# First attention of a two-layer decoder: all four groups in paired steps, the convolution's heads between the turns of the last

## The reference

```python
x = x + L0_attn(layernorm(x))            # 16 heads of 16, LoRA weights, softmax
x = x + L0_xattn(ctx, ctx, layernorm(x)) # long convolution of ctx*ctx products, times q
x = x + L0_ffn(layernorm(x))             # LoRA experts, top 2 of 8
x = x + L1_attn(layernorm(x))            # 16 heads of 128
x = x + L1_xattn(layernorm(x), ctx, mask)
x = x + L1_ffn(layernorm(x))             # 32 routed experts
```

```python
q, k, v = [x @ W.T + b for W, b in ...]          # x: (16, 128, 256), 16 heads of 16
p = softmax(q @ k.T / 4); out = p @ v
x = x + out @ Wo.T + bo
```

## Time and profile before

| | us |
|---|---|
| median of 3 runs (lowest, highest) | 953.66 (953.63, 954.13) |
| the profiled execution | 953.93 |
| its span in the profile | 952.10 |
| TensorE busy in the span | 927.0 (97%) |
| VectorE, ScalarE, GpSimd busy | 620.6, 481.0, 239.7 |

### The profile page before, as it was taken

One profiled execution on the slowest core, in us unless ns is written; L12 is line 12 of the kernel. 1 busy time (PEld: TensorE's weight loads), 2 busy tenths in 40 slices (PEclk: granted clock), 3 DMA queues, 4 the chain that ended last, 5 costly groups with the idle time before them and its releaser, 6 DMA issues.

```text
span 952.1 us, 20014 instructions
## 1 busy us (share of the span) xinstructions
PE 927.0 (97%) x7627; PEld 790.5 (83%) x7627; DVE 620.6 (65%) x1380; ACT 481.0 (51%) x1614; POOL 239.7 (25%) x261
## 2 busy tenths in 40 slices
PE   9999999999999999999999999999999999999988
PEld 7777778899788888888888888888888887777767
DVE  5878777897865576564456464546546665777864
ACT  4988877444445554443444353444444554434632
POOL 2656796671011111111111111011111123101000
PEclk9999999999999999999999999999999999999999
DMA  7100000002430000000000000020003001200002
GB/s 287 68 2 2 2 2 2 2 1 92 136 130 1 2 1 1 1 1 1 1 1 1 2 1 1 1 62 1 1 1 90 1 1 68 113 2 2 2 2 89
DMA packets 11325, 28.02 MB, mean 29 GB/s; under 512 B 1856, under 2 KB 7264, under 8 KB 10720
## 3 DMA queue, kind: packets, MB, share of 16 engines
q1 hardware_dynamic: 10512, 26.48, 7.9%
q10 hardware_dynamic: 720, 0.27, 0.1%
HBM read 24.65 MB, written 2.10 MB: 28 GB/s over the span
## 4 chain that ended last, share of the span: by engine, by line
PE 86%; DVE 9%; issue 2%; ACT 2%; POOL 1%; DVEq 0%; POOLq 0%; ACTq 0%
PE bank L50 15%; PE bank L52 14%; PE bank L51 14%; PE bank L2294 6%; PE bank L2243 5%; PE bank L421 3%; PE bank L431 3%; PE bank L2284 3%; PE bank L2167 2%; PE bank L2158 2%; PE bank L180 2%; PE bank L443 2%; PE bank L1702 2%; PE bank L1133 1%; PE bank L1151 1%
## 5 line engine op out<-in xcount | busy, mean ns | idle before, releaser
L2099 POOL TENSOR_TENSOR wa_prob<-wa_prob,wa_rsum 128x512 f32<-128x512 f32 x64 | 67.6, 1057 | 405.1 <-DVE wa_rsum L2682 405.1
L2476 ACT ACTIVATE wa_prob<-wa_prob,wa_negmax 128x128 f32<-128x128 f32 x256 | 100.1, 393 | 66.5 <-DVE wa_negmax L2671 66.2
L50 PE MATMUL bank<-norm_xT_hi,wide_hi 128*128 128x512 f32 x256 | 105.9, 414 | 0.2 <-DVE norm_xT_lo L191 0.2
L51 PE MATMUL bank<-norm_xT_lo,wide_hi 128*128 128x512 f32 x256 | 101.0, 395 | 0.0
L52 PE MATMUL bank<-norm_xT_hi,wide_lo 128*128 128x512 f32 x256 | 101.0, 395 | 0.0
L2738 DVE TENSOR_TENSOR wa_z_lo<-bank,wa_z_hi 128x512 fp32r<-128x512 f32 x64 | 44.3, 692 | 86.8 <-ACT wa_z_hi L2510 86.3
L646 ACT ACTIVATE v_prob<-bank,la_negmax 128x128 f32<-128x128 f32 x256 | 91.3, 384 | 13.6 <-DVE la_negmax L733 13.6
L2484 ACT COPY wa_q<-bank 128x512 f32<-128x512 f32 x64 | 37.6, 588 | 93.5 <-PE bank L52 93.5
L2491 ACT COPY wa_v<-bank 128x512 f32<-128x512 f32 x64 | 37.4, 586 | 89.2 <-PE bank L52 89.2
L353 POOL TENSOR_TENSOR v_prob<-v_prob,la_rsum 128x512 f32<-128x512 f32 x64 | 66.8, 1043 | 47.2 <-DVE la_rsum L738 47.1
L2294 PEld LDWEIGHTS bank<-wa_probT,wa_v 128*128 128x128 f32 x512 | 65.4, 191 | 10.7 <-DVE wa_probT L2725 5.0
(11 more groups left out here) (287 smaller groups left out, 2363.6 us busy)
## 6 DMA issues: line engine op xcount, KB each, us to landing
wide_raw<-in_wide_w SPq DMA_DIRECT2D x16, 512.0 KB, 6.9
em_w<-in_em_w SPq DMA_DIRECT2D x1, 4096.0 KB, 13.7
lc_kt<-in_ctx_rev SPq DMA_DIRECT2D x1, 2048.0 KB, 10.8
lc_toep<-in_toeplitz SPq DMA_DIRECT2D x1, 2048.0 KB, 14.5
li_kt<-in_ctx_rev SPq DMA_DIRECT2D x4, 512.0 KB, 6.8
out_x<-x SPq DMA_DIRECT2D x8, 256.0 KB, 2.5
x<-in_x SPq DMA_DIRECT2D x3, 512.0 KB, 5.0
h_or_w<-in_li_w SPq DMA_DIRECT2D x1, 1024.0 KB, 5.0
```

The costliest lines, as they stand in the source:

```text
L50: nc.tensor.matmul(out, a[0], b[0], start=start, stop=False, skip_group_check=True)
L51: nc.tensor.matmul(out, a[0], b[1], start=False, stop=False, skip_group_check=True)
L2099: nc.gpsimd.tensor_tensor(prob[:, s], prob[:, s], rsum[:, s, :].unsqueeze(2).to_broadcast([P, G, P]), ALU.mult).then_inc(prob_ok, 1)
L2476: last = nc.scalar.activation(prob[:, s, j, :], prob[:, s, j, :], ACT.Exp, bias=negmax[:, s, j:j + 1], scale=SCALE, accum_out=sums[:, s, j ...
```

## The change

All four groups are now taken in pairs on TensorE. The separate loop for the last group is gone. In a pair of the last group (p = 0 to 7) two convolution heads, 2p and 2p + 1, stand between the two turns, the even one in `b_p[0]`, the odd one in `b_p[1]`. Behind every second pair stands a projection (11 to 14), behind pairs 4 and 6 a turn of x for the convolution stage, all three kinds in `b_p[1]`: so an odd head also waits for the addition to x (`x_ok`) of the projection before it, or for the copy of the turned x. ScalarE copies both heads of a pair in the even step, behind the exponentials.

VectorE's order in the last group becomes that of the others: the copy of the turn first, then the row maximum, which also loses its special place at the start of a group. Additions and the splits of x move by a step at three places. The power and the application of the norm move one step later, (7, 8) to (8, 9), 6 to 7. Eight skips move from group 1 to the last group. In groups 1 and 2 the queries' first product moves from behind pair 0 to between the turns of pair 1, in groups 0 and 1 the first turn of the next x from behind pair 4 to between the turns of pair 5. A projection now comes ahead of what else stands between two turns. In group 0 the second turn of x moves from behind pair 0 to between the turns of pair 1.

```diff
-    STATS_AT, VAR_AT, POWER_AT, APPLY_AT, BIAS_AT = (3, 5), 6, 6, (7, 8), 10
+    STATS_AT, VAR_AT, POWER_AT, APPLY_AT, BIAS_AT = (3, 5), 6, 7, (8, 9), 10
...
-    TURN_0 = (10, 13)
+    TURN_PAIRS = (4, 6)
...
     def hi_due(n):
 
-        return batch_due(n, RG) if n <= PAIRED else batch_due(n, HI_AT) if n > PAIRED + RG else None
+        return batch_due(n, RG)
...
         def between(g, p):
 
             t = g + 1
-            if p == 2:
+            if p == 1 and g > 0:
+                pe.wait_ge(norm.s_lo, DC * norm.split(t))
+                q_or_k(t, 0, 0, b_p[0], q_ps)
+            elif p == 5 and t + 1 < NG:
+                pe.wait_ge(k_ok, DC * t + 2)
+                turn_x(t + 1, 0, b_p[0])
+            elif p == 2:
...
         def first_conv(h):
 
+            p, second = divmod(h, 2)
             if h == 0:
                 pe.wait_ge(v_ok, 2 * NG)
                 pe.wait_ge(kk_first, 2 * CONV_C)
-            else:
-                pe.wait_ge(c_ok, h)
+            wait(pe, c_ok, h - 1)
+            if second:
+                if p - 1 in TURN_PAIRS:
+                    pe.wait_ge(norm.s_hi, DC * (norm.done(NG) - 1) + TURN_PAIRS.index(p - 1) + 1)
+                elif p % 2 == 0:
+                    pe.wait_ge(x_ok, NB - 5 + p // 2)
+                else:
+                    pe.wait_ge(x_ok, NB - 5)
             pe.wait_ge(pr.skip_ok, h + 1)
-            conv_head(pr, 0, h, b_p[0]).then_inc(c_ps, 1)
+            conv_head(pr, 0, h, b_p[second]).then_inc(c_ps, 1)
+
+        def behind_last(p):
+
+            pe.wait_ge(c_ok, 2 * p + 2)
+            if p in TURN_PAIRS:
+                c = TURN_PAIRS.index(p)
+                pe.wait_ge(x_ok, NB - 3 + c)
+                turn_x(NG, c, b_p[1])
+            elif p % 2 == 1:
+                project(NB - 5 + p // 2)
...
-        for n in range(0, PAIRED, 2):
+        for n in range(0, N, 2):
             g, u = divmod(n, U)
             p = u // 2
-            late = n >= 2 * 2
             turn(n)
-            if late:
-                between(g, p)
+            if n == 0:
+                scores(n + RG)
+                pe.wait_ge(v_ok, 1)
+                turn_x(1, 0, b_p[0])
+            elif n == 2:
+                pe.wait_ge(norm.s_lo, DC * norm.split(0) + 1)
+                turn_x(1, 1, b_p[0])
+                scores(n + RG)
+            elif g < NG - 1:
                 b = project_due(n + 1)
                 if b is not None:
                     project(b)
+                between(g, p)
             else:
-                scores(n + RG)
-            if n == 0:
-                pe.wait_ge(v_ok, 1)
-                turn_x(1, 0, b_p[0])
+                first_conv(u)
+                first_conv(u + 1)
             turn(n + 1)
-            if late:
+            if 2 < n < N - RG:
                 scores(n + RG)
             weigh(n)
             weigh(n + 1)
-            behind(g, p)
-        for n in range(PAIRED, N + 1):
...
+            if g < NG - 1:
+                behind(g, p)
+            else:
+                behind_last(p)
...
         def keep_first_conv(h):
             act.wait_ge(c_ps, h + 1)
-            conv_keep(pr, 0, h, b_p[0]).then_inc(c_ok, 1)
+            conv_keep(pr, 0, h, b_p[h % 2]).then_inc(c_ok, 1)
...
-            if N - U < n <= N:
-                keep_first_conv(n - (N - U) - 1)
+            if PAIRED <= n < N and u % 2 == 0:
+                keep_first_conv(u)
+                keep_first_conv(u + 1)
...
-            if g in (1, 2) and u % 2 == 1:
-                if g == 1 and u == 1:
+            if g == 2 and u % 2 == 1:
+                if u == 1:
                     dve.wait_ge(pr.conv_loaded, 16 * 4)
-                add_skip(pr, 8 * (g - 1) + u // 2)
+                add_skip(pr, u // 2)
+            if g == NG - 1 and u < CONV_H // 2:
+                add_skip(pr, CONV_H // 2 + u)
...
-            opens = n < PAIRED and 0 < g and u == 0
-            if n < PAIRED:
+            if n < N:
                 keep_probT(n)
...
-                if n > 1 and n % U == 1:
-                    row_max(n + 2)
-                if not opens:
-                    row_max(n + 3)
+            if n + 3 < N:
+                row_max(n + 3)
...
```

More of the change, by code:

```diff
@@ L494, in behind @@
             t = g + 1
[L495 to L499, removed]
+            if g == 0 and p == 1:
                 pe.wait_ge(norm.s_lo, DC * norm.split(t))
                 q_or_k(t, 0, 0, b_p[0], q_ps)
-            elif p == first + 1:
+            elif p == (2 if g == 0 else 1):
                 pe.wait_ge(q_ok, DC * t + 1)
                 q_or_k(t, 0, 1, b_p[0], k_ps, (0,))
-            elif p == 4 and t + 1 < NG:
-                pe.wait_ge(k_ok, DC * t + 2)
-                turn_x(t + 1, 0, b_p[0])
             elif p == 5:
@@ L585, in tensor_program @@
             weigh(n + 1)
-            behind(g, p)
-        for n in range(PAIRED, N + 1):
[L588 to L597, removed]
-            if PAIRED < n:
-                weigh(n - 1)
-            b = batch_due(n, PROJECT_AT)
-            if b is not None:
-                project(b)
-            if n < N and not first:
-                extra(g, u)
-            if PAIRED < n and u % RG != 1:
-                first_conv(n - PAIRED - 1)
+            if g < NG - 1:
+                behind(g, p)
+            else:
+                behind_last(p)
         pe.wait_ge(exp_ok, N)
@@ L659, in extra @@
             if t == NG:
-                if u - 1 in TURN_0:
-                    norm.hi_chunk(act, NG, TURN_0.index(u - 1), b_p[1], pr.xe)
+                if u // 2 - 1 in TURN_PAIRS and u % 2 == 0:
+                    norm.hi_chunk(act, NG, TURN_PAIRS.index(u // 2 - 1), b_p[1], pr.xe)
                 return
@@ L666, in extra @@
                 norm.hi_chunk(act, t, 1, b_p[0], xT[t % 2][0])
-            elif u == 10 and t + 1 < NG:
+            elif u == 11 and t + 1 < NG:
                 norm.hi_chunk(act, t + 1, 0, b_p[0], xT[(t + 1) % 2][0])
@@ L712, in scalar_program @@
             b = hi_due(n)
-            if b is not None and n <= PAIRED:
+            if b is not None:
                 keep_o(b)
@@ L722, in scalar_program @@
                 extra_late(g, u)
-            b = hi_due(n + 1)
-            if b is not None and n >= PAIRED:
-                keep_o(b)
-            if N - U < n <= N:
-                keep_first_conv(n - (N - U) - 1)
+            if PAIRED <= n < N and u % 2 == 0:
+                keep_first_conv(u)
+                keep_first_conv(u + 1)
     def vector_program(dve, ahead):
@@ L833, in vector_program @@
                     norm.lo_chunk(dve, 1, 0, b_p[0], *xT[1])
-                if n == 3:
+                if n == 2:
                     norm.lo_chunk(dve, 1, 1, b_p[0], *xT[1])
-                if n > 1 and n % U == 1:
-                    row_max(n + 2)
-                if not opens:
-                    row_max(n + 3)
+                if u == 11 and g + 2 < NG:
+                    norm.lo_chunk(dve, g + 2, 0, b_p[0], *xT[g % 2])
+            if n + 3 < N:
+                row_max(n + 3)
             b = hi_due(n)
```

15 lines of the change are left out of this document (2 added, 13 removed).

## The result

| | before | after |
|---|---|---|
| median us (lowest, highest) | 953.66 (953.07, 954.13) | 957.70 (956.97, 958.34) |
| span of the profiled execution | 952.10 | 956.0 |
| TensorE busy | 927.0 | 925.0 |
| VectorE, ScalarE, GpSimd busy | 620.6, 481.0, 239.7 | 620.1, 480.5, 236.7 |

The ratio after to before is 1.0038, 95% interval [1.0027, 1.0049], which does not contain 1. The forecast was 953.6, from 950.6 to 956.2. TensorE is busy for 2 us less and the kernel takes 4 us more, so waits were added.

What follows compares the result with a forecast made beforehand. TensorE was taken to set the pace in the first attention. From 953.93, 2.2 saved in the first three groups, 2.1 lost in the last and 0 behind it gave 953.8, less the profile-to-median difference 953.6 us; range 950.6 to 956.2.

Steps and rivals of the forecast that it cites:

- the front: First three groups: five moves together to save 2.2 us, from 0.6 to 3.0.
- The new waits ahead of heads 5, 9, 13: Last group: these heads wait for the addition emptying their bank, 1.47 each with the fresh start, 4.4 us together.
- TensorE's own work, pairing: Last group: without new waits, paired steps take 35.24 us instead of 38.98, a gain of 3.7.
- the turn of x: Last group, first turn of x behind pair 4: waits 0.9 us for the later normalisation, 0.1 to 1.6.
- Skips "fill VectorE's idle time": Eight skips moved from group 1 to the last group fill VectorE's idle time there, with no cost charged.
- The queries' move: Groups 1 and 2: first product between the turns of pair 1 saves 0.3 us each, 0.6 together.
- The power: Group 0: power at step 7 instead of 6 lets step 8's normalisation go first, saving a 0.5 us GpSimd wait.
- GpSimd's other waits: First three groups: VectorE work moved from ahead of reciprocals saves 0.9 of 1.9 us, from 0 to 1.5.
- The start: Group 0: second turn of x and its split a step earlier, ahead of a maximum, remove a 0.2 us wait.
- Behind the last weighing: VectorE's first convolution product starts 1.7 us after the last weighing, as before: 0, from -0.2 to +1.4.
- B: Last group, slower rival: late head copies on ScalarE delay exponentials and a later turn; 956.4 us, chance 0.22.
- the first three groups saved under 1 us: Sign of error named beforehand: the forecast is wrong if the first three groups save under 1 us.

Runs made afterwards that it cites:

- e1: Changed kernel with VectorE's additions 11 to 13 ahead of the copy of the turn in the last group: 953.08 us.
- e10: e8 with the two weighings of the last group's first six pairs apart, one ahead of the scores and one behind: 953.29 us.
- e6: Changed kernel with the eight skips in group 1 again instead of the last group: 957.21 us.
- e13: Changed kernel with the queries' first product of groups 1 and 2 behind pair 0 again: 956.36 us.
- e2: Changed kernel with the queries' or keys' product ahead of the projection in pairs 1 and 3 of groups 0 to 2: 956.27 us.
- e12: e8 plus the last group's normalisation a step earlier and the last normalisation in halves at steps 14 and 15: 950.58 us.
- e4: The change's new order of the first three groups and its skips, with the last group's order of the kernel before: 954.00 us.
- e3: Changed kernel with GpSimd's products behind the first attention waiting for VectorE's last four normalisations: 957.07 us.
- e8: Changed kernel with additions 11 to 13 ahead of the copy and products ahead of the projection in pairs 1 and 3: 951.57 us.
- e5: Changed kernel with the last group's power and normalisation halves one step earlier: 957.20 us.

## Why the prediction was wrong

The waits foreseen for the last group came. What failed is the front: it was to save 2.2 us and saved nothing. Against the forecast of -0.1 stand +4.0: of the 4.1 between them, 2.3 are the front's, 1.4 the last group's, 0.3 came behind the last weighing, and 0.1 is the later first turn.

1. **The new waits ahead of heads 5, 9, 13 (priced 4.4): right.** 1.35 each in the trace and 1.59 with the late head's fresh start, 4.8 for the three (0.4 over the price); 4.6 us back in e1. That they would last under 0.7, a sign of being wrong, did not come.
2. **TensorE's own work, pairing (priced 3.7 saved): right where it can be read alone.** Pairs 2 and 5 took 4.10 in e1 for 4.11, and the price of a changed tile shape is there in e10. The group of e1 is 38.2 and not 35.2 because of what stood in it: 1.2 at the turn of x (priced 0.9; 0.94 in the changed kernel), 0.8 instead of 0.4 at a weighing, 0.7 of the skips, in which the one wait for GpSimd of 0.26 is contained, and some 0.8 that is spread over the pairs and not assigned.
3. **Skips "fill VectorE's idle time" (priced 0): failed.** They cost 0.7 us in the first four pairs (e6). The rows of the kernel before showed normalisations that took 1.53 and 0.85 at two places; the same contention should have been charged to every VectorE operation moved beside GpSimd's products.
4. **The queries' move (priced 0.6 saved): the step that failed in the front.** It cost 0.5 a group instead, 1.0 in all; undone it gave 1.3 (e13). The sum had the projection at 0.82 wherever it stood, and counted only the wait of 0.17 of the turn behind it. The wait that it would meet with nothing in front of it, for VectorE's addition of the projection before, was not asked for: 0.64. The same omission in pair 3, ScalarE's copy of the queries, cost 0.5 (e2), and there the sum had no term at all. Even with the wait covered the saving of 0.3 a group is not there: e2 loses 0.1 a group.
5. **The power (0.5) and GpSimd's other waits (0.9): right in size.** From turn 4 to turn 8 the changed kernel wins 0.6, from turn 19 to 27 it wins 0.9. Of the latter 0.7 come from the skips that left group 1 (e6 wins only 0.25 there), the same 0.7 that they cost in the last group: their move is worth nothing. **The start (0.2): absent**; a weighing of pair 1 in group 0 waits 0.85 where it waited 0.43.
6. **Behind the last weighing (0, up to +1.4): 0.3.** The products start 3.0 us behind the weighing's end instead of 1.7, close to the upper bound, and then run faster, 1.84 against 2.37, and the ones behind them too. e12 shows what the place was worth.

The front's sum is -0.6 -0.9 +1.0 +0.5 +0.1 = +0.1, by the trace 0.05 from first turn to turn 48, and e4 says 954.0. The last group's is 3.4 instead of 2.1: 0.7 for the skips, 0.4 at the three heads, the rest small. Of the rivals, B gave the right side for another reason and too little: no trace shows a turn late for exponentials behind ScalarE's head copies, and the turns behind the stalled pair 2 come at the same distances as in e1, which has no stall (2.39 us to turn 55 in both). That the first three groups saved under 1 us was named as a sign of error, and it is what came.

## What to carry to other kernels

When a step is moved ahead on an in-order engine, everything that now stands behind a shorter stretch has to be asked again what it waits for: here the projection lost its cover twice. Before two banks are shared between two streams, put the operation that frees the bank first on its engine; three additions placed behind a copy cost 4.6 us, and placed ahead of it no head waited for them. And an operation that is free by idle time is not free beside another engine that slows it: take its duration from a row where both run.

## What the hardware showed

**VectorE and GpSimd slow each other, and it depends on the operation.** Alone a skip takes 0.34 us and four normalisations 1.37; beside GpSimd's products up to 1.06 and 3.01 (3.54 in e1). Copies from a bank of 0.69 stay 0.69 there (e12). GpSimd is slowed as well: its six products behind the attention take 5.2 us beside the normalisations in the changed kernel, and 7.5 beside VectorE's first products in e3 (384 columns: 0.87 and 1.47 us). The Trainium skill (SBUF — State Buffer, "Who interferes with whom") says that a VectorE instruction with two inputs in SBUF contends with a GpSimd one that reads SBUF: the skips agree. By its words an instruction with one SBUF input contends only in the two-port modes, which it says tensor_scalar can enter. The normalisations are tensor_scalar, with one tensor and two columns of scalars from SBUF, and were slowed 2.2 times, which fits; no run here says in which mode they ran.

**The granted clock can fall behind short waits, in some executions only.** e10's profiled execution, windows of 2 us (length, busy TensorE, its weight loads, VectorE, ScalarE, GpSimd, clock):

```profile
155.00:157.00 2.00, 1.70 (x32) 1.13 (x24) 1.58 (x5) 1.31 (x8) 1.54 (x2) 1.00 0.03 8
157.00:159.00 2.00, 1.14 (x8) 1.17 (x9) 0.80 (x4) 0.48 (x1) 1.24 (x3) 0.84 0.00 0
159.00:161.00 2.00, 2.00 (x10) 2.00 (x9) 1.63 (x4) 1.71 (x10) 0.54 (x1) 0.50 0.00 0
161.00:163.00 2.00, 2.00 (x20) 1.63 (x20) 0.85 (x3) 1.10 (x6) 1.52 (x2) 0.80 0.00 0
```

Behind the wait of 1.16 us at the turn of x the clock goes from 2.4 to 1.2 GHz for some three us and comes back; from turn 58 to turn 59, with two heads, it is 3.58 us instead of the 1.91 of e8. In e5's profile the idle time is 1.72 us, ahead of head 9, and the clock is 0.50 from 160 to 165 us. But the three waits of 1.35 in the changed kernel, and those of 1.17 at the turn of x in e1 and e8, leave it at 1.00. The single executions of e1, e4, e5, e8 and e10 with a mean clock of 0.996 to 0.998 are 0.8 to 2.5 us above the median of their kernel, and three such of the kernel before, whose last group has no wait above 0.80, some 2. So such a wait may cost more than it lasts, in an execution now and then; that the wait is the cause is not shown, and what decides when is open.
